# Two seams of an attention stage: group 1 turned later, the first projection and its scaling ahead of the last update, the masked keys ahead of groups 4 to 7

## What is computed

```python
x = x + 0.5 * _L0_ffn_ref(_layernorm(x), ...)
x = x + _L0_attn_ref(_layernorm(x), ...)
x = x + 0.5 * _L0_ffn_ref(_layernorm(x), ...)

def _L0_ffn_ref(x, Win, bin_, W1, b1, W2, b2, Wout, bout):
    s = x @ Win + bin_                              # 64 features
    h = relu(s[..., None] * W1 + b1)                # 16 values for each of them
    g = einsum('btmh,mh->btm', h, W2) + b2
    return g @ Wout + bout

def _L0_attn_ref(x, W_qkv, ln_gamma, ln_beta, W_proj, b_proj):   # windows of 64, 16 heads of 8
    q, k, v = split(x @ W_qkv)
    q = _layernorm(q, ln_gamma, ln_beta); k = _layernorm(k, ln_gamma, ln_beta)   # over the 8
    attn = softmax(einsum('bqhd,bkhd->bhqk', q * SCALE, k))
    return (attn @ v) @ W_proj + b_proj
```

## Time and profile before

| | |
|---|---|
| median of 3 executions | 1345.27 us (1343.96 to 1350.82) |
| the profiled execution: time / span | 1348.92 us / 1347.1 us |
| its mean granted TensorE clock | 0.941 |
| busy: TensorE, VectorE, ScalarE, GpSimd | 1148.4, 1087.4, 911.0, 724.0 us |
| feed-forward 0, up to the first projection | 0 to about 90 us |
| first seam | about 75 to 118 us |
| pairs of the attention | about 118 to 288 us |
| second seam | about 288 to 320 us |
| second feed-forward | about 304 to 377 us |
| product keys, second attention, product keys | 377 to 1347 us |

### The profile page before, as it was taken

One profiled execution on the slowest core, in us unless ns is written; L12 is line 12 of the kernel. 1 busy time (PEld: TensorE's weight loads), 2 busy tenths in 40 slices (PEclk: granted clock), 3 DMA queues, 4 the chain that ended last, 5 costly groups with the idle time before them and its releaser, 6 DMA issues.

```text
span 1347.1 us, 55515 instructions
## 1 busy us (share of the span) xinstructions
PE 1148.4 (85%) x22892; PEld 946.2 (70%) x22892; DVE 1087.4 (81%) x4029; ACT 911.0 (68%) x2131; POOL 724.0 (54%) x655
## 2 busy tenths in 40 slices
PE   2767888887748999999998679999658999999996
PEld 1654666656727888888888347777437888888886
DVE  4967888858788989989994568888688899999981
ACT  3854555638647888878885436666558888888881
POOL 4215545433046878878775500000148788788882
PEclk9888999978969999999999979999769999999999
DMA  6000000000002222222222000000002222222223
GB/s 164 20 1 1 2 2 2 2 1 1 1 0 52 60 49 47 47 47 63 47 48 50 1 1 1 0 0 1 1 16 51 59 52 47 47 61 50 47 64 80
DMA packets 27568, 43.41 MB, mean 32 GB/s; under 512 B 6960, under 2 KB 18480, under 8 KB 27440
## 3 DMA queue, kind: packets, MB, share of 16 engines
q1 hardware_dynamic: 27440, 41.82, 13.8%
HBM read 6.15 MB, written 2.10 MB: 6 GB/s over the span
## 4 chain that ended last, share of the span: by engine, by line
PE 52%; DVE 10%; issue 9%; ACT 3%; DMA 2%; SPq 2%; POOL 1%; POOLq 0%; DVEq 0%
PE bank L1878 22%; PE bank L1889 7%; PE bank L1860 7%; PE bank L1851 4%; DMA rowsD<-work 2%; PE bank L1762 2%; DVE work L974 2%; SPq L333 2%; PE bank L1744 1%; DVE work L1016 1%; PE bank L1465 1%; PE bank L1707 1%; PE bank L1723 1%; PE bank L1677 1%; PE bank L1778 1%
## 5 line engine op out<-in xcount | busy, mean ns | idle before, releaser
L1878 PEld LDWEIGHTS bank<-rowsD,work 128*32 128x32 f32 x16384 | 360.5, 194 | 58.1 <-issue 57.6
L1878 PE MATMUL bank<-rowsD,work 128*32 128x32 f32 x16384 | 371.1, 275 | 23.1 <-issue 14.9
L443 POOL TENSOR_SCALAR work<-work 128x1024 f32<-128x1024 f32 x64 | 181.5, 2837 | 127.3 <-ACT work L1338 127.2
L431 POOL TENSOR_TENSOR work<-work 128x512 f32<-128x512 f32 x128 | 167.9, 1336 | 27.2 <-ACT work L1363 26.2
L1338 ACT ACTIVATE work<-work 128x128 f32<-128x128 f32 x512 | 163.3, 412 | 1.9 <-DVE work L1036 1.9
L1346 ACT ACTIVATE work<-work 128x128 f32<-128x128 f32 x512 | 158.2, 398 | 6.0 <-DVE work L1046 6.0
L445 POOL TENSOR_TENSOR work<-work 128x1024 f32<-128x1024 f32 x64 | 152.5, 2383 | 5.3
L1016 DVE STREAM_TRANSPOSE work<-work 128x1024 f32<-128x1024 f32 x128 | 151.2, 1220 | 1.8 <-ACT work L1346 1.8
L1363 ACT ACTIVATE work<-bank 128x512 f32<-128x512 f32 x128 | 77.8, 617 | 91.5 <-PE bank L1878 91.2
L356 POOL TENSOR_SCALAR xn<-x_sb,negmean,rstd 128x128 f32<-128x128 f32 x58 | 32.5, 564 | 186.5 <-DVE shift L595 133.9
L1889 PE MATMUL bank<-kout,work 128*128 128x128 f32 x1024 | 128.1, 278 | 2.8 <-POOL work L431 2.8
(11 more groups left out here) (199 smaller groups left out, 2321.1 us busy)
## 6 DMA issues: line engine op xcount, KB each, us to landing
rowsD<-work SPq DMA_DIRECT2D x256, 128.0 KB, 2.4
x_sb<-in_L_attn_x_dram SPq DMA_DIRECT2D x8, 256.0 KB, 4.7
out_dram<-x_sb SPq DMA_DIRECT2D x4, 512.0 KB, 5.3
headsel<-in_c_headsel_dram SPq DMA_DIRECT2D x1, 512.0 KB, 4.3
work<-in_L_ffn_key_in_dram SPq DMA_DIRECT2D x1, 512.0 KB, 7.9
kout<-in_L_ffn_key_out_dram SPq DMA_DIRECT2D x4, 128.0 KB, 5.1
work<-in_L_ffn_keys_dram SPq DMA_DIRECT2D x1, 256.0 KB, 3.0
wqkv<-in_L_attn_W_qkv_dram SPq DMA_DIRECT2D x1, 192.0 KB, 4.2
```

The costliest lines, as they stand in the source:

```text
L431: last = nc.gpsimd.tensor_tensor(cg[:, par, :].rearrange("p (j t) -> p j t", j=NCH)[:, :, half * 64:half * 64 + 64], csb[:, par, 512 * hal ...
L443: nc.gpsimd.tensor_scalar(wmask, both, 1.0 - 5e-7, None, ALU.is_ge).then_inc(s["wm"], 1)
L1878: last = nc.tensor.matmul(bank[2 + half][k * NK:(k + 1) * NK, :] .rearrange("p (j t c) -> p t c j", j=NCH, t=16)[:, t % 16, :, :], xrows[: ...
```

## The change

It writes a few steps in another place on four engines; no operation is added or removed. At the end of the first feed-forward, group 1 of the norm is turned and copied after the last hidden vectors and not ahead of them; VectorE does the update of group 6 and its half of group 1 ahead of the last `sums`; TensorE does the projection of pair 0 ahead of the last `project_out`. VectorE does the scaling of pair 0 ahead of the update of group 7. TensorE turns q and k of pair 0 right after group 2. GpSimd makes the masked keys of pair 0 ahead of its share of groups 4 to 7, and these groups are turned in two halves, after the first scores of pair 0 and at the end of `sequence(-1)`. At the second seam, groups 0 and 1 are normed, turned and copied half a pair earlier, and VectorE's aggregate for groups 6 and 7 and its share of group 3 come after the first `sums`.

```diff
@@ gpsimd, head_keys_0
-                for n in range(2, NG):
-                    ln_normalise(1, n)
+                ln_normalise(1, 2)
+                ln_normalise(1, 3)
                 pool.wait_ge(s_w, 16 * NW)
                 for u in range(-2, NP_):
                     sequence(u, u % 2)
+                    if u == -2:
+                        for n in range(4, NG):
+                            ln_normalise(1, n)
@@ vector, ffn
                 if f == 1:
                     ln_normalise(2, 2)
+                sums(0, 0)
+                if f == 1:
                     ln_normalise(2, 3)
-                sums(0, 0)
+                    ln_aggregate(2, SPLIT[2])
...
-                        if g == 5:
-                            ln_normalise(1, 1)
...
-                sums(NG - 1, 1)
-                ffn_update(f, NG - 2)
-                if f == 1:
+                if f == 0:
+                    ffn_update(f, NG - 2)
+                    ln_normalise(1, 1)
+                    sums(NG - 1, 1)
+                else:
+                    sums(NG - 1, 1)
+                    ffn_update(f, NG - 2)
                     ffn_update(f, NG - 1)
@@ vector, l0
                     less_max(u + 1, 1)
+                    if u == NP_ - 1:
+                        ln_normalise(2, 0)
+                        ln_normalise(2, 1)
                     update(u - 1)
...
+                spread(0)
                 ln_normalise(1, 2)
-                ln_normalise(1, 3)
-                spread(0)
+                scale(0)
                 ffn_update(0, NG - 1)
                 ln_aggregate(1, SPLIT[1])
-                scale(0)
+                ln_normalise(1, 3)
                 ln_finish(1, SPLIT[1])
...
                 sequence(NP_ - 1, 1)
-                ln_normalise(2, 0)
-                ln_normalise(2, 1)
                 sequence(NP_, 0)
-                ln_aggregate(2, SPLIT[2])
@@ scalar, ffn
                     if f == 0 and g == 6:
                         ln_evacuate(1, 0)
-                        ln_evacuate(1, 1)
@@ scalar, l0
+                    if u == NP_ - 1:
+                        ln_evacuate(2, 0)
+                        ln_evacuate(2, 1)
                     evacuate(u, 1, 1)

                 squares(0)
+                ln_evacuate(1, 1)
                 ln_normalise(1, 2)
+                roots(0)
                 ln_normalise(1, 3)
-                roots(0)
                 ln_evacuate(1, 2)
-                ln_evacuate(1, 3)
-                ln_root(1, SPLIT[1])
                 keys(0)
                 queries(0, 0)
+                ln_root(1, SPLIT[1])
+                ln_evacuate(1, 3)
                 ln_normalise(1, 4)
                 ln_normalise(1, 5)
-                for n in range(4, NG):
-                    ln_evacuate(1, n)
-                    if n + 2 < NG:
-                        ln_normalise(1, n + 2)
-                for u in range(-1, NP_ - 1):
+                ln_evacuate(1, 4)
+                ln_normalise(1, 6)
+                ln_evacuate(1, 5)
+                ln_normalise(1, 7)
+                sequence(-1, 1)
+                ln_evacuate(1, 6)
+                ln_evacuate(1, 7)
+                for u in range(NP_ - 1):
                     sequence(u, u % 2)
@@ tensor, ffn
                     if f == 0 and g == NG - 1:
                         ln_turn(1, 0)
-                        ln_turn(1, 1)
...
+                if f == 0:
+                    ln_turn(1, 1)
+                    project_first()
                 project_out(NG - 1, 1)
@@ tensor, l0, in sequence(u) and ahead of it
                     scores(u + 1, 1 - par, 0)
+                    if u == -1:
+                        ln_turn(1, 4)
+                        ln_turn(1, 5)
...
                     turn_qk(u + 2)
+                    if u == NP_ - 1:
+                        ln_turn(2, 0)
+                        ln_turn(2, 1)
                     weigh(u, par, 0)
...
                     weigh(u, par, 1)
+                    if u == -1:
+                        ln_turn(1, 6)
+                        ln_turn(1, 7)
...
                 ln_turn(1, 2)
+                turn_qk(0)
                 ln_turn(1, 3)
-                sequence(-2, 0)
-                for n in range(4, NG):
-                    ln_turn(1, n)
+                project_pair(1, 1)
```

36 lines of the change are left out of this document (16 added, 20 removed).

## The result

The changed kernel took 1338.69 us in the median of 11 runs (1336.34 to 1340.82); the kernel before, beside it on the same chips, took 1349.01 us in 11 runs (1342.62 to 1353.58), some 3.7 us more than the three runs shown ahead. The ratio, taken between executions timed side by side, is 0.9928 [0.9913, 0.9943]: 9.7 us faster (7.7 to 11.7); the two medians lie 10.3 apart. The profiled execution took 1340.82 us, its span is 1339.0 us, 8.1 less than that of before.

What follows compares the result with a forecast made beforehand. The prediction took no engine as full and the seams, where engines wait for each other, as the bound. First seam 3.4 plus second 3.8 gave 7.2 us, from the median 1345.27 to 1338.1, predicted as 1338.0 us, range 1332.5 to 1343.5.

Steps and rivals of the forecast that it cites:

- First seam, 3.4 forecast: From the end of the first feed-forward into the first pair: 3.4 us won, 2.0 to 5.2.
- TensorE no longer waits either: End of the first feed-forward: project_out of group 6 starts at 77.4, when its sums end, and lasts 3.7 us.
- only about 0.4 of the 1.2: First pair: of 1.2 us for the copies of groups 6 and 7 on ScalarE, only about 0.4 shows as loss.
- the text's own bound of 113: First seam: masked keys of pair 1 later than 113 would show the prediction wrong; 110 to 111.5 right.
- 1.1 of the 4.7 us: First seam: values started 4.7 us after the squares; 1.1 goes because the scores of pair 0 are done earlier.
- Second seam, 3.8 forecast: Last pair into the second feed-forward: 3.8 us won, 2.5 if norms cost more, up to 6.5 at 2.4 GHz.
- The 0.4 us put down as lost: Second seam, ahead of the first weigh: VectorE's norm beside GpSimd's share, and the turns, lose 0.1 to 0.8, taken as 0.4.
- The 1.4 are given back: Second feed-forward: 1.4 us saved ahead of the first sums is lost to group 3's norm and turn before project_out.
- Low ends: Rival, both seams: half clock in the first, slow norms in the second; 4.5 us won, 1340.8 us; chance 0.27.
- Full clock through both seams: Rival: TensorE stays at full clock in both seams; 11.3 us won, 1334.0 us; chance 0.17.
- The clock in the pair loop: Rival, attention pairs: the clock falls, some 3 us per pair; five pairs make it slower, 1353 us; chance 0.06.
- GpSimd holding VectorE: Rival, first seam: pair 0's masked keys hold off VectorE's aggregate; the kernel wins 2.5 us, 1342.8 us; chance 0.10.

Runs made afterwards that it cites:

- seam1_only: The changed kernel with the second seam's moves taken back on VectorE, ScalarE and TensorE; ratio 0.998 to the kernel before.
- seam2_no_dve: The changed kernel with VectorE's aggregate and group 3 put back ahead of the second feed-forward's first sums; ratio 0.9949 to the kernel before.
- keys_late: The changed kernel with groups 4 to 7 normed, turned and copied first again, ahead of pair 0's masked keys on GpSimd; ratio 0.9907 to the kernel before.
- scale_early: The changed kernel with the scaling of pair 1 taken ahead of the turns of groups 4 to 7; ratio 0.9908 to the kernel before.
- sums_first: The changed kernel with VectorE's last sums ahead of group 6's update and TensorE's last project_out ahead of group 1's turn; ratio 0.993 to the kernel before.
- scale_early_sums: sums_first with the scaling of pair 1 also taken ahead of the turns of groups 4 to 7; ratio 0.9888 to the kernel before.
- seam2_only: The kernel before with only the second seam's moves on VectorE, ScalarE and TensorE; ratio 0.9949 to the kernel before.
- fill_seam1: The changed kernel with idle transposes in three of TensorE's gaps in the first seam; ratio 0.9917 to the kernel before.
- fill_all: fill_seam1 with two more stretches of idle transposes, one in the second feed-forward; ratio 0.9903 to the kernel before.

## Why the prediction came out right, step by step

- **The time.** 1338.69 against 1338.0, but by a larger gain from a slower start: 9.7 where 7.2 was forecast, and the kernel before took 1349.01 beside it and not 1345.27. The three runs of before were too few to place its median. With the right one the same sum gives 1341.8, 3.1 us above the measured time: that the level came out to 0.7 us is luck, two errors that cancel. The gain itself, 7.2, lies just below the interval of 7.7 to 11.7.
- **First seam, 3.4 forecast, 2.7 measured alone.** The interval, 0.8 to 4.4, holds both the forecast and its low end. The wait of ScalarE went as said, and the order of TensorE too. But "TensorE no longer waits either" was wrong: it waits 2.1 us for the last hidden vectors ahead of `project_out`, and what that does to the clock was put at nothing. `project_out` at "3.7 us" held where the clock did (3.8 in `seam1_only`) and was 5.4 in the changed kernel's profile. Seven profiled executions have this wait, with the same instructions of TensorE around it and no idle transposes: the clock fell in three (changed, `seam2_no_dve`, `keys_late`) and held in four (`seam1_only`, `scale_early`, `sums_first`, `scale_early_sums`). It costs 3.2 us at the masked keys of pair 0 (26.9 and 23.7 from the table's start).
- **First seam, the rest.** With the clock up, `turn_qk` of pair 0 and the masked keys of pairs 0 and 1 came at 92.11, 93.36 and 111.39 (`seam1_only`), within 0.5 us of what the forecast has; in the changed kernel's profile they came at 94.19, 95.43 and 113.28, and the seam won 0.4 us up to pair 2, below the forecast's range. The term "only about 0.4 of the 1.2" came out in the changed kernel (0.3) as the sum of two larger ones: the squares of pair 2 start 1.59 us after the masked keys of pair 1 in the old kernel (116.11) and 3.52 in the new one (116.80), behind the copies of groups 6 and 7; against that, `scale` of pair 2, now later, no longer has a step of 2.42 us beside GpSimd's addition; its longest small step is 0.80 (118.83). In `seam1_only` 1.9 are given back, with the scores at 1.2 GHz.
- **Masked keys of pair 1.** At 110 to 111.5 in the forecast; 111.39 in `seam1_only`, 113.28 in the changed kernel, which by the text's own bound of 113 would have been wrong. That 1.1 of the 4.7 us between the squares and the values of pair 0 would go held (104.50 to 108.13, 3.6). But the masked keys of pair 0 ahead of groups 4 to 7 show no gain in `keys_late`, and `scale_early` shows that the scaling of pair 1, behind the turns of groups 4 and 5, was the chain.
- **Second seam, 3.8 forecast, 6.9 measured alone.** In the profile 7.5 at the first hidden vector and 1.2 behind it. The move closed the gap as said: of the 6.8 us won between the start of `outputs` and the first vector (11.0 before, 4.2 after) 3.5 are the gap, where 3.4 were forecast. The other 3.3 are shorter products. So mis-sized is the clock: the forecast's high end, 6.5 us for TensorE at 2.4 GHz, was the case here, in every profile that has the move. The 0.4 us put down as lost ahead of it were a gain of 0.6. That `seam2_only`, with the old first seam, wins the same 7.5 and 1.2 says that it is a property of the seam. "The 1.4 are given back" was right for the start of `project_out` (8.50 and 8.66 us after the first vector), and missed the earlier rise of the clock inside it, 1.6 us.
- **The rivals.** Low ends: not of the second seam; of the first the time cannot tell (2.7 lies between 2.0 and 3.4). Full clock through both seams: true of the second alone. The clock in the pair loop: not in the changed kernel, whose pairs from 2 to 15 take 143.7 us where they took 143.6; in `fill_seam1` and `scale_early_sums` it fell in one pair, for 1.6 us. GpSimd holding VectorE: VectorE of the changed kernel beside the masked keys of pair 0:

```profile
95.58 0.44 DVE L571 TENSOR_TENSOR negmean<-stats 128x16 f32<-128x16 f32 x1
95.94 0.17 DVE L572 TENSOR_TENSOR mdiff<-stats 128x16 f32<-128x16 f32 x1
...
96.25 0.35 DVE L575 TENSOR_SCALAR negmean<-negmean 128x16 f32<-128x16 f32 x1
...
96.78 0.34 DVE L581 TENSOR_TENSOR vareps<-vareps,mdiff 128x16 f32<-128x16 f32 x1
97.05 0.76 DVE L605 TENSOR_SCALAR xn<-x_sb,negmean,rstd 128x128 f32<-128x128 f32 x2
```

The seven operations of the aggregate take from 95.58 to 97.12, 1.5 us where 0.9 were allotted, each held for 0.2 or 0.3 at most. So VectorE comes in between GpSimd's masked keys, and the strong form of the rival is refuted: it costs 0.6 us at the aggregate, and not the 4.6 that the rival put on group 3. The Trainium skill, "SBUF — State Buffer", section "SBUF: two separate sides", has the lock held for one instruction; beside the masked keys the trace agrees. In the earlier trace rows it does not: the step of VectorE that starts at 118.42 lasts until 120.84, over two copies of GpSimd and the addition behind them.

```profile
118.78 0.41 POOL L380 COPY work<-xT 128x256 f32<-128x256 f32 x1
119.12 0.41 POOL L387 COPY work<-xT 128x256 f32<-128x256 f32 x1
```

Why VectorE gets in between the masked keys and not between the copies and the addition is open.

What stays open is why the granted clock falls in three of seven executions after a wait of the same length. `seam2_no_dve` and `keys_late`, where it fell, ran on one chip, and the four where it held on two others; the chip of the changed kernel's profile is not known, so a difference between chips is not excluded. Open too is how much of the 6.2 us that `fill_all` wins in its profile up to pair 2 is in its usual executions; its time shows 3.4 us in all, not clear of the noise.

## What to carry to other kernels

When a wait is taken out of a seam, ask what the next instruction on the waiting engine needs: here the masked keys were made early, and the scaling of the next pair, one line further down on ScalarE, was the chain; putting that first won 5.7 us (`scale_early_sums` against `sums_first`), while no gain of the early keys shows. A gap of 1.5 us on TensorE in a sparse stretch is priced with the products behind it, at their length at 1.2 GHz; closing it was worth 6.9 us here where the forecast had 3.8. And time the kernel before as often as the changed one: three runs placed its median 3.7 us low.

## What the runs showed of the hardware that I had not expected

Behind the same wait of 2.1 us and the same instructions, the granted clock fell to 1.2 GHz in three profiled executions (six products 1.49 us) and stayed at 2.4 GHz in four (0.83 us). With 12 idle transposes in that wait, which leave 0.8 us of it, it stayed up in all three profiles that have them. In the old kernel, eight transposes ahead of a gap of 1.54 us did not hold it over that gap. In the last pair, whose instructions and gaps are the same up to there, it was 0.72 over 12 us in eight profiles and 1.00 in five. A VectorE step of 128x64 stood 2.42 us beside two copies and an addition of GpSimd, and none of the aggregate's steps was lengthened by more than 0.3 us beside GpSimd's eight masked keys.
